# A four-layer graph network on one core: casting DMAs for the adjacency, eleven-block groups in the first layer, and paired row maxima in the second

## The chip, the core and the metric

The kernel runs on one core of one Trainium2 chip. The metric is device time in microseconds (us) of one execution; lower is better. TensorE is called PE below, VectorE DVE, ScalarE ACT, GpSimd POOL, and SyncE SP. SP issues nearly all DMAs of the kernel before.

## The reference, cut to what matters

The input is x (2708 x 256) and a 0/1 adjacency matrix adj (2708 x 2708, diagonal 1). Each of four layers computes `h = relu(layernorm(x))` and adds the result of a graph layer to x.

```
# layer 0: attention with 4 heads of 64 columns
ht = (h @ Wm) per head; el = ht.al; er = ht.ar
scores = leaky_relu(el[i] + er[j], 0.2), -inf where adj[i, j] == 0
x += softmax(scores) @ ht
# layer 1: two GRU cells and 3 attention heads; D = diag(adj), A = adj without its diagonal
edge_output = gru(A @ h, h)
hW = h @ W[k]; e = leaky_relu((A @ hW) . a)           # one score per node
support = mean over k of (softmax_j(e[j] where A[i, j] > 0) * A) @ hW
x += D * edge_output + D * gru(support, h)
# layer 2
x += concat(h, adj @ h / (deg + 1)) @ W2.T
# layer 3: its weights are not zero only where adj < 1 is not 0; for this input a flag skips it
```

## The kernel before, in words

Nodes are padded to 2816 = 22 tiles (`NT`) of 128. AT holds adj transposed in fp8, for all 22 source tiles j; most other buffers lie in one `arena` that the stages use in turn.

**Start.** DVE, ACT and PE normalise x and form ht and the two scores. SP loads adjT in 32-bit chunks into four staging buffers (`STG`), and POOL casts them into AT (L690 for the first six target blocks, L714 for the rest). Between the first casts POOL also splits six weight pieces into fp16 halves (L673 to L675). Then a chain over the 22 tiles forms MOV, the moving operand of layer 0: POOL L704 and DVE L1161 make the products, ACT L856 and DVE L1167 split them in two fp16 parts.

**Layer 0.** leaky_relu has two pieces, so exp of a score is a product of a row factor and a column factor, with different factors on either side of the threshold el + er > 0. A unit is (group g of target blocks, head h): `GA` has groups of 6, 8 and 8 blocks, thus 12 units. For each unit and each source tile j a threshold tile is made (0 or 1 in fp8 over the group's columns) by ACT as a steep sigmoid (L866), or for `j % 7 == 3` by DVE (L1183). DVE ands it with the AT words (`positive_mask`, L1215) and xors for the complement (`other_mask`, L1221), 4 bytes per word, into a ring of `NMASK` = 12. PE multiplies each mask block with MOV (L1677, 65 columns, 4 matmuls per block and tile j) into one PSUM bank per block. The first four and last four tiles j of a unit are taken together (`rounds(4)`). At j = 8 of the next unit ACT scales each bank by the row factors into E (`evict`, L878, two instructions a block), and two masks later DVE adds, divides and adds to X (`head_out`, L1230 to L1236). DVE also widens AT from 1 to 1.875 (`widen`, L1242), and POOL clears AT's diagonal blocks (L720).

**Before layer 1.** After the last unit: head_out, the last 8 blocks' `norm_stats` and `norm_scales` (L1084 to L1106), then a chain per tile: ACT norm (L824), POOL fp16 part (L727), DVE rest (L1284), PE transposes (L1694). ACT may start block t >= 8 only when SP has saved block t - 8 to DRAM (L515, one of eight buffers).

**Layer 1, edge GRU.** For each tile t PE does the support A @ h (L1723), the three heads' products (L1735, L1737) and the gates (L1768, L1775). ACT and DVE split the products (`products_low`, L1358), which PE waits for before the next tile's products. DVE also takes row maxima, `row_max`, one per head, tile and half row (132 in all, L1373): SP loads 1408 columns of adj in 32 bits (L506, three buffers `AROW`), POOL clears the diagonal block (L748), and DVE multiplies with the scores in EB and takes the maximum. 44 maxima of head 0 are spread over tiles 0 to 12 and 29 of head 1 over tiles 14 to 21; the other 59 lie in the attention stage.

**Layer 1, attention.** Nine units (3 heads x 3 groups). ACT or DVE make exponents (L960, L1416) from the row maxima MB, DVE masks them (L1426), ACT turns them into powers (L969), PE multiplies (L1818, L1819). MB comes from DRAM (`m_rows`): PE turns the maxima, DVE copies them (L1386), SP saves them (L542) and loads them broadcast (L551). The last stages are the node GRU, layer 2's linear part, and the neighbours' sum (L1872).

SP's program is one order of loads and waits; a wait holds up all that SP issues behind it. [The functions that the change touches follow.]

Of the kernel before, what the change touches and what calls it, by code (L numbers as in the profile page):

```python
# [6 lines left out]
F32 = mybir.dt.float32  # L7
# [8 lines left out]
P = 128  # L16


def gnn_stack_kernel(nc, t_in, out):
# [14 lines left out]
    H1 = 3  # L34
# [6 lines left out]
    GA = [(0, 6), (6, 8), (14, 8)]  # L41
# [3 lines left out]
    EVICT_AT = 8  # L45
    NTHR = 6
    NORM0_SPLIT = 4
    LOG2E = 1.0 / float(np.log(2.0))
# [5 lines left out]
    NORM1 = [(0, 14), (14, NT)]  # L54
# [8 lines left out]
    ROWS_SPLIT = 13  # L63
    ROWS_EDGE = 73
# [12 lines left out]
    with ExitStack() as ctx:  # L77
# [53 lines left out]
        THR = a0.take(NTHR, 1024, dt=FP8, size=1)  # L131
        mask_at = a0.at
        MASK = a0.take(NMASK, 2, 1024, dt=FP8, size=1)
        stg_at = a0.at
        STG = a0.take(4, 1024)
        stg_end = a0.at
        ELB = a0.take(2, 1024)
        e_at = a0.at
        E = a0.take(8, 2 * C0)
# [16 lines left out]
        RD = a0.take(8)  # L156
# [4 lines left out]
        assert a0s.at <= stg_at  # L161
        GWT = THR.rearrange("p a b -> p (a b)").bitcast(F32).rearrange("p (a b) -> p a b", b=D)
        htf_at = GA[0][1] * P
        HTF = AT[:, :, htf_at:htf_at + 4 * H0 * C0].bitcast(F32)
        THRi = THR.bitcast(mybir.dt.int32)
# [8 lines left out]
        EB = a1.take(N)  # L174
        AROW = a1.take(3, QUARTER)
        rows_end = a1.at
        NSH = a1.take(2, DC, 2, 2 * P, dt=F16, size=2)
        assert a1.at >= stg_at
        WIHS = a1.take(DC, 2, 3 * D, dt=F16, size=2)
        WHHS = a1.take(DC, 2, 3 * D, dt=F16, size=2)  # L180
        assert a1.at <= stg_end
# [4 lines left out]
        ah.at = late_at  # L186
        H32R = ah.take(8, D)
# [80 lines left out]
        M2 = sb("M2", [P, NT, 2, H1])  # L268
# [4 lines left out]
        KM = ln[:, 5, :]  # L273
# [4 lines left out]
        MN_D = nc.dram_tensor("m_rows", [H1, NT, P], F32, kind="Internal").ap()  # L278
        HT_D = nc.dram_tensor("h_turned", [P, NT, 4 * P], F16, kind="Internal").ap()
# [11 lines left out]
        banks_before = []  # L291
        cnt = 0
        for g, h in units0:
            banks_before.append(cnt)
            cnt += GA[g][1]
        banks_before.append(cnt)
        stg_before = [16 * len(range(q, len(chunk0), 4)) for q in range(4)]

        def threshold_on_act(n, j):

            if n == 0:
                return True
            return j % 7 != 3

        act_thr, dve_thr = [0], [0]
        for n in range(len(units0)):
            for j in range(NT):
                on_act = threshold_on_act(n, j)
                act_thr.append(act_thr[-1] + on_act)
                dve_thr.append(dve_thr[-1] + (not on_act))  # L310
# [37 lines left out]
        casts_at = {}  # L348
        n = NT
        for u, count in enumerate((6, 6, 5, 5, 6, 6, 5, 5)):  # L350
            for i in range(count):
                casts_at[(u, 1 + 4 * i if i < 2 else 10 + 3 * (i - 2))] = n
                n += 1
        assert n == len(chunk0)

# [4 lines left out]

        def rows_before(t):

            if t <= ROWS_SPLIT:
                return -(-2 * NT * t // ROWS_SPLIT)
            if t >= NT:
                return ROWS_EDGE
            return 2 * NT + max(0, -(-(ROWS_EDGE - 2 * NT) * (t - ROWS_SPLIT - 1) // (NT - ROWS_SPLIT - 1)))

        row_at = {2 * i: ROWS_EDGE + i for i in range(2 * NT * H1 - ROWS_EDGE)}
# [4 lines left out]
        def row_of(L):  # L374

            h, i = divmod(L, 2 * NT)
            return h, i // 2, i % 2
# [11 lines left out]
        first_count = [[0], [0], [0]]  # L389
        for m in range(3 * 3 * NT):  # L390
            for e in range(3):
                first_count[e].append(first_count[e][-1] + (first_of(m) == e))
        first_sem = ["y_act", "y_dve", "y_pool"]
# [20 lines left out]
        def _(sp):  # L414
# [4 lines left out]
            def load_chunk(n):  # L419
                g, j = chunk0[n]  # L420
                b0, nb = GA[g]
                if 4 <= n < NT + 4:
                    sp.wait_ge(sem("stg_cast"), n - 3)
                if n >= NT + 4:
                    sp.wait_ge(sem("stg_used"), n - 3 - NT)
                sp.dma_start(STG[:, n % 4, 0:nb * P], adjT[j, :, b0 * P:(b0 + nb) * P]
                             ).then_inc(sem(f"stg{n % 4}"), 16)

            def load_el(n):
                g, h = units0[n]  # L430
                b0, nb = GA[g]
                if n >= 2:
                    sp.wait_ge(sem("t_act"), act_thr[(n - 1) * NT])
                    if dve_thr[(n - 1) * NT] > 0:
                        sp.wait_ge(sem("t_dve"), dve_thr[(n - 1) * NT])
                sp.dma_start(ELB[:, n % 2, 0:nb * P].rearrange("p (k q) -> p k q", q=P),
                             EL_D[b0:b0 + nb, h, :].partition_broadcast(P)).then_inc(sem(f"elb{n % 2}"), 16)
# [17 lines left out]
            for n in range(4):  # L455
                load_chunk(n)
# [6 lines left out]
            for n in range(4, NT):  # L463
                load_chunk(n)
                i, odd = divmod(n - 5, 2)
                if odd == 1 and 0 <= i < len(pieces):
                    sp.wait_ge(sem("ws"), i + 1)
# [1543 lines left out]
```

## Time and profile before

| | |
|---|---|
| median of 3 runs | 1348.96 us (1347.34 to 1359.39) |
| the profiled execution's own time | 1352.68 us |
| its span, first to last instruction | 1350.9 us |
| PE, DVE, ACT, POOL busy | 1147.0, 975.3, 808.1, 322.4 us |
| mean granted clock of TensorE | 0.934 |

The profile is of one execution. Its own time is 1.8 us longer than its span and 3.7 us above the median. In it x = 0 is the first instruction; the stages follow each other at about 0 to 98 (start), 98 to 389 (layer 0), 389 to 450 (norm and scores of layer 1), 450 to 709 (edge GRU), 709 to 1068 (attention), 1068 to 1250 (node GRU) and 1250 to 1351 us (neighbours' sum).

### The profile page before, as it was taken

Reading aid. Unit: us, or ns where it says so; the run is one execution under the profiler, and the core shown is the slowest. Engines: PE = TensorE matmul, PEld = TensorE weight load, DVE = VectorE, ACT = ScalarE, POOL = GpSimd, SP = SyncE. Lnnn points to the kernel's source line nnn. Section 1 sums busy time; section 2 is a strip of 40 time slices with the busy share of each in tenths; the row PEclk is TensorE's granted clock in tenths of the full one; section 3 lists DMA queues with packets and bytes.
Section 4 is the critical chain, followed back from the end, with each engine's and each line's share of the span. In section 5 each row is a group of like instructions: output and inputs, shape, how many; then the busy total and the mean of one; then the engine's idle time right before and its main releaser. Section 6 shows DMA issues by size and latency. Waiting matters only on the chain.

```text
span 1350.9 us, 35958 instructions
## 1 busy us (share of the span) xinstructions
PE 1147.0 (85%) x15055; PEld 940.4 (70%) x15055; DVE 975.3 (72%) x2219; ACT 808.1 (60%) x1232; POOL 322.4 (24%) x383
## 2 busy tenths in 40 slices
PE   4518888999867999899966999999899997778997
PEld 3418888999757767666635888887788663445886
DVE  6599897899983577776786999897996365553541
ACT  3468889999753223223325999997989465653000
POOL 4862313133032032333231121111211042220000
PEclk9759999999975999999987999999899998899999
DMA  9734535111016577777779778776762010020532
GB/s 315 244 137 122 179 126 191 36 35 66 4 57 230 160 237 240 240 252 253 266 265 347 221 272 325 240 249 222 255 222 112 1 32 17 16 94 1 174 127 85
DMA packets 89465, 225.10 MB, mean 167 GB/s; under 512 B 7521, under 2 KB 52689, under 8 KB 89041
## 3 DMA queue, kind: packets, MB, share of 16 engines
q1 hardware_dynamic: 88113, 222.21, 48.8%
q8 instruction: 120, 1.97, 0.6%
q10 hardware_dynamic: 1184, 0.53, 0.1%
q14 instruction: 48, 0.39, 0.1%
HBM read 202.98 MB, written 19.73 MB: 165 GB/s over the span
## 4 chain that ended last, share of the span: by engine, by line
PE 38%; DVE 23%; DMA 17%; ACT 8%; issue 7%; POOL 5%; SPq 2%; DVEq 0%; ACTq 0%; POOLq 0%
DMA arena<-in_adj 14%; PE PS L1872 8%; PE PS L1818 7%; PE PS L1819 7%; PE PS L1677 6%; DVE scratch L1373 5%; DVE arena L1215 4%; PE PS L1768 3%; DVE arena L1221 3%; ACT arena L866 2%; PE PS L1859 2%; DVE arena L1161 2%; PE PS L1775 1%; ACT arena L878 1%; POOL arena L748 1%
## 5 line engine op out<-in xcount | busy, mean ns | idle before, releaser
L1818 PE MATMUL PS<-arena 128*128 128x257 f16 x1452 | 331.5, 276 | 21.4 <-ACT arena L969 14.7
L1819 PE MATMUL PS<-arena 128*128 128x257 f16 x1452 | 331.3, 277 | 0.0
L1677 PE MATMUL PS<-arena 128*128 128x65 f16 x7744 | 259.4, 195 | 75.8 <-DVE arena L1221 61.0
L1677 PEld LDWEIGHTS PS<-arena 128*128 128x128 fp8e4 x7744 | 255.3, 99 | 79.9 <-issue 58.0
L1373 DVE CUSTOM_DVE_ANT_0 scratch<-arena 128x1408 bf16<-128x1408 f32 x132 | 216.0, 1636 | 76.7 <-DMA arena<-in_adj 39.8
L866 ACT ACTIVATE arena<-arena 128x1024 fp8e4<-128x1024 f32 (+1 forms) x231 | 227.9, 1085 | 23.0 <-DVE arena L1215 22.5
L969 ACT ACTIVATE arena<-arena 128x896 int16<-128x896 uint8 (+1 forms) x198 | 187.6, 973 | 31.6 <-DVE arena L1426 22.3
L1818 PEld LDWEIGHTS PS<-arena 128*128 128x128 bf16 x1452 | 144.3, 99 | 47.4 <-ACT arena L969 13.6
L1819 PEld LDWEIGHTS PS<-arena 128*128 128x128 bf16 x1452 | 141.5, 97 | 23.0
L960 ACT ACTIVATE arena<-arena,E1B 128x896 uint8<-128x896 f32 (+1 forms) x131 | 139.3, 1064 | 12.7 <-DMA arena<-m_rows 12.7
L1215 DVE TENSOR_TENSOR arena<-arena,AT 128x256 int32<-128x256 int32 (+1 forms) x264 | 114.7, 434 | 26.2 <-ACT arena L866 26.1
L948 ACT ACTIVATE arena<-arena 128x256 f32<-128x256 f32 x44 | 18.3, 417 | 179.6 <-DVE arena L1397 179.6
L1768 PE MATMUL PS<-arena 128*128 128x512 f16 x528 | 122.9, 383 | 0.3 <-ACT PS L932 0.3
L1221 DVE TENSOR_TENSOR arena<-arena,AT 128x256 int32<-128x256 int32 (+1 forms) x264 | 116.3, 441 | 0.0
L748 POOL TENSOR_TENSOR arena<-arena,NOTI 128x128 f32<-128x128 f32 x66 | 47.3, 716 | 275.6 <-DMA arena<-in_adj 275.6
L1723 PE MATMUL PS<-AT,arena 128*128 128x256 fp8e4 x968 | 111.8, 276 | 0.0
L1872 PE MATMUL PS<-arena,AT 128*128 128x256 f16 x968 | 106.2, 273 | 0.8 <-DVE X L1523 0.8
L1723 PEld LDWEIGHTS PS<-AT,arena 128*128 128x128 f16 x968 | 95.6, 99 | 12.2
L1872 PEld LDWEIGHTS PS<-arena,AT 128*128 128x128 fp8e4 x968 | 94.6, 98 | 12.5 <-DVE X L1523 1.1
L733 POOL TENSOR_TENSOR arena<-arena 128x256 f32<-128x256 f32 x44 | 33.5, 761 | 258.1 <-ACT arena L948 258.1
L1768 PEld LDWEIGHTS PS<-arena 128*128 128x128 f16 x528 | 52.0, 99 | 57.3 <-issue 3.6
L1426 DVE TENSOR_TENSOR arena<-arena,AT 128x224 int32<-128x224 int32 (+1 forms) x198 | 82.3, 441 | 11.3 <-ACT arena L960 11.3
(187 smaller groups left out, 1537.8 us busy)
## 6 DMA issues: line engine op xcount, KB each, us to landing
arena<-in_adj SPq DMA_DIRECT2D x176, 704.0 KB, 5.4
arena<-in_adjT SPq DMA_DIRECT2D x44, 512.0 KB, 7.5
hw_saved<-arena SPq DMA_DIRECT2D x22, 387.0 KB, 7.2
arena<-in_adjT SPq DMA_DIRECT2D x22, 384.0 KB, 5.4
arena<-hw_saved SPq DMA_DIRECT2D x9, 774.0 KB, 7.9
arena<-h_saved SPq DMA_DIRECT2D x44, 128.0 KB, 2.1
arena<-e_rows SPq DMA_DIRECT2D x3, 1408.0 KB, 7.2
arena<-el_rows SPq DMA_DIRECT2D x8, 512.0 KB, 5.5
```

What stands on the lines that cost most here:

```text
L866: act.activation(THR[:, m % NTHR, 0:nb * P], ELB[:, n % 2, 0:nb * P], ACT.Sigmoid, bias=ERB[:, j, h:h + 1], scale=SHARP, saturate=False).t ...
L960: act.activation(Y[:, m % NRING, 0:nb * P], MB[n % 2][:, 0:nb * P], ACT.Relu, bias=E1B[:, j * H1 + h:j * H1 + h + 1], saturate=False).then ...
L969: act.activation(PWb[:, m % NRING, 0:nb * P], Y[:, m % NRING, 0:nb * P], ACT.Copy, scale=256.0).then_inc(sem("p_ready"), 1)
L1215: dve.tensor_tensor(mask_words(m, 0), THRi[:, m % NTHR, 0:GA[g][1] * P // 4], adj_words(m), ALU.bitwise_and).then_inc(sem("m_plus"), 1)
L1221: dve.tensor_tensor(mask_words(m, 1), mask_words(m, 0), adj_words(m), ALU.bitwise_xor).then_inc(sem("masks_built"), 1)
L1373: dve.tensor_tensor_reduce(junk, AROW[:, L % 3, :], eb[:, c * QUARTER:(c + 1) * QUARTER], 1.0, 0.0, ALU.mult, ALU.max, M2[:, t, c, h:h + 1 ...
L1677: ins = pe.matmul(PS[:, k, q * C0:(q + 1) * C0], MASK[:, (m + j) % NMASK, q, k * P:(k + 1) * P], MOV[:, j, 2 * h + q, a, :], start=(j == 0 ...
L1723: ins = pe.matmul(PS[:, c, 0:D], HHL[:, j, a, c * P:(c + 1) * P], AT[:, j, i0 * P:i1 * P], start=(j == 0 and a == 0), stop=(j == NT - 1 an ...
L1768: ins = pe.matmul(PS[:, bank, :], half(c, a), w[:, c, b, 0:2 * D], start=False, stop=(w is wih and c == DC - 1 and a == 1), skip_group_che ...
L1818: pe.matmul(PS[:, k, 0:D + 1], weights, w[:, 0:D + 1], start=(j == 0), stop=False)
L1819: ins = pe.matmul(PS[:, k, 0:D + 1], weights, w[:, D + 2:2 * D + 3], start=False, stop=(j == NT - 1))
L1872: ins = pe.matmul(o, AT[:, j, t * P:(t + 1) * P], YHL[:, j, a, :], start=(j == 0 and a == 0), stop=(j == NT - 1 and a == 1))
```

## The change

- **Loads.** Staging and POOL's casts go. POOL issues DMAs that cast while they move: 22 of adjT's first 11 blocks per tile (32 bits to fp8) at the start, 22 of the other 11 blocks, each after every third mask (masks 1 to 64), and then 22 DRAM-to-DRAM copies of adj's rows into a bf16 array `AH_D`, one every fourth mask from mask 68 to 152. POOL's six weight splits come after the first 22 issues. SP waits for the 22 copies, then writes zeros on the diagonal of AH_D with one DMA of 127 x 22 elements of 2 bytes, and waits for that too. Behind these waits on SP's queue are the loads of the GRU weights, the biases and the saves of h (L515).
- **Layer 0.** Two groups of 11 blocks, 8 units. A unit uses one of two sets of four PSUM banks, three blocks to a bank. ACT takes all 176 thresholds of 1408 columns and no evictions. DVE takes the masks of 352 words and, at j = 13, four evictions (three blocks each, one multiplication by a broadcast factor) and head_out for 11 blocks. The diagonal is cleared by two DVE ands at the end. After the last unit eviction, head_out and norm_stats go bank by bank; 11 blocks' norm_stats stand there instead of 8.
- **Row maxima.** One bf16 half row (352 KB, two buffers) serves heads 0 and 1: 44 loads for 88 maxima, spread over tiles 0 to 19 of the edge GRU; the maxima of both are turned and saved together. Head 2's 44 maxima and loads lie in the attention stage, at every 2.25th mask, and are turned at unit 5, j = 0 instead of j = 13. POOL's clearing of rows goes. The 26 checks in the attention stage have own buffers.

```diff
-    GA = [(0, 6), (6, 8), (14, 8)]
+    GA = [(0, 11), (11, 11)]
...
-    EVICT_AT = 8
+    EVICT_AT = 13
+    PER_BANK = 3
+    L0_BANKS = 4
...
-    NORM1 = [(0, 14), (14, NT)]
+    NORM1 = [(0, 11), (11, NT)]
...
-    ROWS_SPLIT = 13
-    ROWS_EDGE = 73
+    ROWS_LAST = 20
...
+        EB = a1.take(2, N)
+        AROW = a1.take(2, QUARTER, dt=BF16, size=2)
...
         def rows_before(t):
+            return min(PAIRED, -(-PAIRED * t // ROWS_LAST))
...
+        row_at = {8 + 9 * i // 4: 2 * NT + i for i in range(2 * NT)}
...                                                       SP
-            sp.wait_ge(sem("stg_used"), len(chunk0) - NT)
+            sp.wait_ge(sem("rows_h"), 16 * NT)
+            sp.dma_start(AH_D.rearrange("t p n -> (t p n)")[0:(P - 1) * NT * (N + 1)]
+                         .rearrange("(a b c) -> a b c", b=NT, c=N + 1)[:, :, 0:1],
+                         ZB[0:P - 1, :].unsqueeze(2), allow_slow_non_contiguous=True).then_inc(sem("rows_z"), 16)
+            sp.wait_ge(sem("rows_z"), 16)
             for i in range(4):
                 sp.wait_ge(sem(f"ws_out{i}"), 16 * len(range(i, len(pieces), 4)))
-            load_halves(WIHS, 1, "we")
-            load_halves(WHHS, 2, "we")
...
-            sp.wait_ge(sem("x_l0"), len(units0))
+            sp.wait_ge(sem("x_l0"), FULL0)
+            load_halves(WIHS, 1, "we")
+            load_halves(WHHS, 2, "we")
             load_bias(BIAS, BRB, "edge_bih", "edge_bhh", "be")
...
-                if L >= 3:
-                    sp.wait_ge(sem("rmax"), L - 2)
-                sp.dma_start(AROW[:, L % 3, :], t_in["adj"][t * P:(t + 1) * P, c * QUARTER:(c + 1) * QUARTER]
+                if L >= 2:
+                    sp.wait_ge(sem("rmax"), maxima_after(L - 2))
+                sp.dma_start(AROW[:, L % 2, :], AH_D[t, :, c * QUARTER:(c + 1) * QUARTER]
...
-                if n == 5 and j == 15:
-                    save_maxima(2)
+                if n == 5 and j == 2:
+                    save_maxima(2, 1)
...                                                       POOL
             for t in range(NT):
-                pool.wait_ge(sem(f"stg{t % 4}"), 16 * (t // 4 + 1))
-                pool.tensor_copy(AT[:, t, 0:GA[0][1] * P], STG[:, t % 4, 0:GA[0][1] * P], saturate=False
-                                 ).then_inc(sem("stg_cast"), 1)
...
+                pool.dma_start(AT[:, t, 0:GA[0][1] * P], adjT[t, :, 0:GA[0][1] * P]).then_inc(sem("adj_a"), 16)
+            for i in range(len(pieces)):
+                pool.wait_ge(sem(f"raw{i % 4}"), 16 * (i // 4 + 1))
+                if i >= 4:
+                    pool.wait_ge(sem(f"ws_out{i % 4}"), 16 * (i // 4))
+                split(RAW[:, i % 4, :], HALF[:, i % 4, :, :], pieces[i][3], 3 * D)
...
+            for t in range(NT):
+                pool.wait_ge(sem("masks_built"), 3 * t + 1)
+                pool.dma_start(AT[:, t, GA[0][1] * P:NT * P], adjT[t, :, GA[0][1] * P:NT * P]).then_inc(sem("adj_b"), 16)
+            for t in range(NT):
+                pool.wait_ge(sem("masks_built"), 68 + 4 * t)
+                pool.dma_start(AH_D[t], t_in["adj"][t * P:(t + 1) * P, :]).then_inc(sem("rows_h"), 16)
...                                                       DVE
+                dve.wait_ge(sem("t_act"), m + 1)
+                if h == 0 and j == 0:
+                    dve.wait_ge(sem(["adj_a", "adj_b"][g]), 16 * NT)
...
+            def evict(n, i):
...
+                dve.tensor_tensor(E[:, k0:k1, :].rearrange("p k (q c) -> p k q c", c=C0),
+                                  PS[:, first_bank(n) + i, 0:nb * 2 * C0].rearrange("p (k q c) -> p k q c", q=2, c=C0),
+                                  coef.to_broadcast([P, nb, 2, C0]), ALU.mult).then_inc(sem("bank_free"), 1)
...
+                if n >= 1 and j == EVICT_AT:
+                    for i in range(L0_BANKS):
+                        evict(n - 1, i)
+                    head_out(n - 1, 0, 11, L0_BANKS)
...
+            dve.tensor_tensor(blocks, blocks, not_diagonal.unsqueeze(1).to_broadcast([P, NT - 1, P // 4]), ALU.bitwise_and
+                              ).then_inc(sem("diag0"), 1)
...
+            for i in range(L0_BANKS):
+                k0, k1 = bank_blocks(i)
+                evict(len(units0) - 1, i)
+                head_out(len(units0) - 1, k0, k1, i + 1)
+                dve.wait_ge(sem("x_l0"), len(units0) + i)
+                for k in range(k0, k1):
+                    norm_stats(1, GA[1][0] + k)
...
+            def row_max(i):
+                if i < PAIRED:
+                    L, h = divmod(i, 2)
+                    eb = EB[:, h, :]
+                else:
+                    L, h = i - 2 * NT, 2
+                    eb = EB2
...                                                       PE
+                    for k in range(11):
+                        i, r = divmod(k, PER_BANK)
+                        if js[0] == 0 and n >= 2 and r == 0:
+                            pe.wait_ge(sem("bank_free"), L0_BANKS * (n - 2) + i + 1)
...
-                    if (n, js[-1]) in ((1, 12), (5, 9)):
+                    if (n, js[-1]) == (4, 19):
```

## Rows read from the trace of the kernel before

**Rows 1.** Busy time by stage: us, each engine's busy (count), PEclk, DMA share, GB/s

```profile
194.00:389.00 195.00, 177.48 (x5312) 175.40 (x5309) 176.38 (x465) 173.30 (x265) 50.38 (x35) 0.96 0.18 60
450.00:709.00 259.00, 233.14 (x1680) 164.71 (x1677) 186.11 (x339) 75.14 (x170) 72.60 (x95) 0.97 0.75 249
709.00:738.00 29.00, 17.53 (x108) 13.17 (x109) 16.19 (x29) 15.30 (x17) 4.88 (x8) 0.71 1.02 358
936.00:958.00 22.00, 14.98 (x110) 11.51 (x108) 16.40 (x35) 15.20 (x16) 3.34 (x3) 0.84 0.80 297
958.00:980.00 22.00, 22.00 (x200) 19.20 (x198) 22.00 (x35) 21.30 (x23) 5.12 (x3) 1.00 0.76 250
```

**Rows 2.** The same view for L1677 alone (PE, PEld), two 4 us windows of layer 0

```profile
234.00:238.00 4.00, 4.00 (x86) 4.00 (x83) 0.57 0.51 151
242.00:246.00 4.00, 4.00 (x132) 4.00 (x129) 1.00 0.01 4
```

**Rows 3.** ACT's timeline: start, us, what, forms, count [idle before]

```profile
91.28 13.41 ACT L866 ACTIVATE arena<-arena 128x768 fp8e4<-128x768 f32 x16
262.43 13.62 ACT L866 ACTIVATE arena<-arena 128x1024 fp8e4<-128x1024 f32 x13
205.60 3.35 ACT L878 ACTIVATE arena<-PS,arena 128x65 f32<-128x65 f32 x16
```

**Rows 4.** DVE's timeline: two masks back to back, and the last mask of layer 0

```profile
203.07 0.42 DVE L1215 TENSOR_TENSOR arena<-arena,AT 128x256 int32<-128x256 int32 x1
203.41 0.43 DVE L1221 TENSOR_TENSOR arena<-arena,AT 128x256 int32<-128x256 int32 x1
382.85 0.42 DVE L1221 TENSOR_TENSOR arena<-arena,AT 128x256 int32<-128x256 int32 x1
```

**Rows 5.** DVE's timeline: first of head_out, first norm_stats, variance, first of the chain

```profile
389.62 0.70 DVE L1230 TENSOR_TENSOR arena<-arena 128x520 f32<-128x520 f32 x1 [3.46 <-ACT arena L878]
392.25 0.43 DVE L1084 BATCH_NORM_STATS2 scratch<-X 128x6 f32<-128x256 f32 x1
396.62 0.17 DVE L1091 TENSOR_SCALAR ln<-mv 128x8 f32<-128x8 f32 x1
398.34 0.42 DVE L1284 TENSOR_TENSOR arena<-arena 128x256 f16<-128x256 f32 x1
```

**Rows 6.** POOL's timeline: last constant, one weight split, first product of the MOV chain

```profile
16.35 0.29 POOL L687 CAST identh<-ident 128x128 f16<-128x128 f32 x1
20.24 0.84 POOL L673 TENSOR_SCALAR arena<-arena 128x768 f32<-128x768 f32 x1 [2.06 <-DMA arena<-in_gatW]
23.63 0.82 POOL L690 CAST AT<-arena 128x768 fp8e4<-128x768 f32 x1
60.52 1.77 POOL L704 TENSOR_TENSOR arena<-AT,arena 128x260 f32<-128x260 f32 x3
```

**Rows 7.** SP's timeline, a load's issue; DMA view, 8 to 10 us, ACT's queue

```profile
0.73 0.45 SPq L416 DMA_DIRECT2D X<-in_x  x1
...
q10 hardware_dynamic: 181, 0.00, 4.9%
```

**Rows 8.** Who waited for whom in the edge GRU: us, times, longest

```profile
PE PS L1735 <- DVE arena L1358: 25.6, 12, 4.5
DVE scratch L1373 <- DMA arena<-in_adj: 38.5, 13, 4.7
```

**Rows 9.** Timeline of the edge GRU: PE's products of two tiles, a second maximum

```profile
560.17 0.39 PE L1735 MATMUL PS<-arena 128*128 128x512 f16 x1 [1.94 <-DVE arena L1358]
570.85 0.39 PE L1735 MATMUL PS<-arena 128*128 128x512 f16 x1
579.97 1.62 DVE L1373 CUSTOM_DVE_ANT_0 scratch<-arena 128x1408 bf16<-128x1408 f32 x1 [0.17 <-DVE M L1373]
```

**Rows 10.** Attention: PE's first matmul (timeline), a save of maxima (chain of waits)

```profile
716.65 0.38 PE L1818 MATMUL PS<-arena 128*128 128x257 f16 x1 [7.94 <-ACT arena L969]
...
929.15 3.84 DMA m_rows<-ET
```

More of the change, by code:

```diff
@@ L155, in gnn_stack_kernel @@
         ELT = a0.take(P)
-        RD = a0.take(8)
+        RD = a0.take(11)
+        ZB = a0.take(NT, dt=BF16, size=2)
+        NOTB = a0.take(P, dt=FP8, size=1)
         a0s = Arena()
@@ L290, in gnn_stack_kernel, with bank_blocks, first_bank @@
         chunk3 = [(g, j) for g in range(len(G0)) for j in range(NT)]
[L291 to L310, printed above, removed]
+        FULL0 = len(units0) + L0_BANKS - 1
+        def bank_blocks(i):
+            return PER_BANK * i, min(PER_BANK * (i + 1), 11)
+        def first_bank(n):
+            return L0_BANKS * ((n + 1) % 2)
+        stg_before = [0] * 4
         norm_parts = {0: NORM0, 1: NORM1, 2: NORM2, 3: [(0, NT)]}
@@ L1257, in _ @@
                     widen(j - 2, 1)
[L1258 to L1259 removed]
                 if m >= 1:
                     other_mask(m - 1)
[L1262 to L1263 removed]
+                if n >= 1 and j == EVICT_AT:
+                    for i in range(L0_BANKS):
+                        evict(n - 1, i)
+                    head_out(n - 1, 0, 11, L0_BANKS)
                 if n == len(units0) - 2 and 3 <= j < 3 + NORM1[0][1]:
                     if j == 3:
[L1266 removed]
+                        dve.wait_ge(sem("x_l0"), H0)
                     norm_stats(1, j - 3)
@@ L1270, in _ @@
             other_mask(last)
+            norm_scales(1, 0)
             dve.wait_ge(sem("masks_built"), last + 1)
@@ L1273, in _ @@
                 widen(t, 1)
-            norm_scales(1, 0)
-            head_out(len(units0) - 1)
-            dve.wait_ge(sem("x_l0"), len(units0))
-            for t in range(*NORM1[1]):
-                norm_stats(1, t)
+            dve.wait_ge(sem("widened"), 2 * NT)
+            not_diagonal = NOTB.bitcast(mybir.dt.int32)
+            flat = AT[:].rearrange("p t n -> p (t n)").bitcast(mybir.dt.int32)
+            blocks = flat[:, 0:(NT - 1) * (N + P) // 4].rearrange("p (t c) -> p t c", t=NT - 1)[:, :, 0:P // 4]
+            dve.tensor_tensor(blocks, blocks, not_diagonal.unsqueeze(1).to_broadcast([P, NT - 1, P // 4]), ALU.bitwise_and
+                              ).then_inc(sem("diag0"), 1)
+            block = flat[:, (NT - 1) * (N + P) // 4:NT * N // 4]
+            dve.tensor_tensor(block, block, not_diagonal, ALU.bitwise_and).then_inc(sem("diag0"), 1)
+            for i in range(L0_BANKS):
+                k0, k1 = bank_blocks(i)
+                evict(len(units0) - 1, i)
[3 more added lines that the diff above has]
+                    norm_stats(1, GA[1][0] + k)
             norm_var(1, 1)
@@ L1388, in gru_new, with maxima_turned @@
+            def maxima_turned(h, heads, bank):
+                dve.wait_ge(sem("eT_mm"), 2 if h < 2 else 3)
+                dve.wait_ge(sem("ep") if h == 0 else sem("mn"), 16)
+                dve.tensor_copy(ET[0:heads * NT, :], PS[0:heads * NT, bank, 0:P]).then_inc(sem("mt"), 1)
             def gru_new(t, base, trz, gt):
```

333 lines of the change are left out of this document (113 added, 220 removed).

## The prediction

> **What bounds the kernel now.** I read the stages first (busy time by stage), then the timelines of the engines in each. In layer 0 no engine is idle for long: in 194 to 389 us, eight units of 8 blocks, PE is busy 177, DVE 176 and ACT 173 of 195 us, 24.4 us a unit [rows 1]. Undisturbed, PE does 132 matmuls in 4 us, 30.3 ns each; in the window after a gap the granted clock is 0.57, near the lower level of 1.2 GHz, and it does 86, 46.5 ns each [rows 2]. A unit of 8 blocks needs 704 matmuls, 21.3 us at full clock. ACT needs 19 thresholds at 13.62/13 = 1.05 us and 16 evictions in 3.35 us, 23.3 us [rows 3]. So ACT sets the pace, and the stage runs 24.4/23.3 = 1.045 times slower than ACT's work.
>
> In the edge GRU PE is busy 233 of 259 us, and 25.6 us of its waits are for DVE's split of the products (L1358), which is late because DVE stood at row maxima whose row was not there [rows 1, 8]. In the attention PE is nearly full, except in two places: 709 to 738 us, with DMA at 1.02 and 358 GB/s, and 936 to 958 us, where it waits for the maxima of head 2 [rows 1, 10].
>
> **Layer 0, the thresholds.** From 768 to 1024 columns a threshold goes from 13.41/16 = 0.84 to 1.05 us; 384 columns more make 1.363. 22 are 30.0 us a unit [rows 3]. ACT loses all evictions. **PE:** 968 matmuls a unit, the total stays 7744, 29.3 us [rows 2]. It no longer waits for evictions, having a second set of banks. **DVE:** masks of 256 words follow each other by 0.34 us; 352 words make at most 0.46 (in proportion), I take 0.44. 44 are 19.4. Four evictions of at most 390 columns: a 520-column add takes 0.70, so about 0.5 each, 2.0. head_out took 392.25 - 389.62 = 2.63 us for 8 blocks, 3.5 for 11 [rows 4, 5]. Together 24.9 us. Widening adds 7 x 0.45 = 3.1 in units 4 to 6. Unit 6 also has 11 norm_stats at (396.62 - 392.25)/8 = 0.55, thus 34.0; unit 7 has 22 widenings, 34.8 [rows 5]. So ACT leads in units 0 to 5, DVE in 6 and 7: 6 x 30.0 + 68.8 = 249 us, times 1.045 = 260. Before, from the first threshold at 91.28 to the last mask at 383.3, it was 292.0 [rows 3, 4]. With 1.4 for the first threshold: **31 us gained**; 42 if the factor is 1. A window at the low clock costs PE 46 matmuls, 1.4 us; two in each unit make 22 us, of which PE's lead of 0.7 us a unit covers 6, and the gain is 15 [rows 2].
>
> **After layer 0.** Before, the first step of the tile chain (L1284) came 15.1 us after the last mask [rows 4, 5]. Now DVE has norm_scales, two widenings and the two ands (about 4 us), then per bank an eviction (0.5), head_out of three blocks (five short operations, 1.6) and three norm_stats (1.65), 3.75 x 3 + 2.8, then variance and scales, 398.34 - 396.62 = 1.7. Sum 20: **5 us lost**. PE's last round (176 matmuls, 8.2 us at 46.5 ns) lies beside it. POOL's clearing of AT was off this path, so its end gives nothing.
>
> **The start.** POOL comes to the MOV chain at 60.5 us now; its inputs would allow about 55. It will issue 22 casting loads from 16.6 us on, then six splits of 3.4 us (20 us) [rows 6]. The trace has no DMA issued by POOL. An issue on SP takes 0.45 us [rows 7]; as low bound 16.6 + 10 + 20 = 47, 5 us gained; a split is three POOL instructions, 1.1 us each, and the high bound is twice that: 16.6 + 48 + 20 = 85, 24 lost. I take the 1.1 us of the same engine: 61 us, plus waits for pieces: **3 lost**. The 22 loads read 15.9 MB. At the 358 GB/s of the saturated stage [rows 1] they take 44 us and end near 61 to 75 beside the other loads; they delay the first mask only under about 215 GB/s. The second 22 have 88 masks (some 125 us), and are hidden. On POOL's queue nothing is behind them but the row copies.
>
> **Row copies and diagonal.** 31.7 MB are read and 15.9 written between masks 68 and 152, about 195 to 322 us, 250 GB/s of reads; the last lands near 328. Then come 2794 elements of 2 bytes. ACT's small loads (4 bytes) held the engines 4.9% of 16 x 2 us for 181 packets, 8.7 ns each [rows 7]: 2 us over 16 engines, 24 us on one. The saves of h wait behind on SP, and ACT's ninth block needs the first at about 374 us. So 46 us, 16.5 ns a packet, are free: **0**, low bound 0. A 2-byte write to DRAM is not in the trace; at five times the read price on one engine it takes 122 us, 76 lost. I stay with the packets' own row. The Trainium skill (DMA: Bandwidth & Descriptors, "Why a DMA increments its semaphore by 16 and not by 1") says that the number of engines is the largest up to 16 that divides the slowest dimension, and 127 partitions go to one. By that rule the zeros take the 24 us rather than 2; no row here shows it. "Specifications" there adds that transfers under 512 bytes are read-modify-write; no row prices that either.
>
> **Edge GRU.** A tile that did not wait took PE 570.85 - 560.17 = 10.7 us; 22 are 235 against 259 [rows 1, 9]. Loads fall from 73 of 704 KB to 44 of 352, so rows will be there. But DVE's maxima rise from 73 to 88, 4.4 a tile at 1.62 to 1.79 us [rows 9], 7.3 us; bf16 input alone I count at nothing, since the scores stay 32 bits. DVE's other work was 186.1 - 73 x 1.7 = 62, 2.8 a tile [rows 1, 9], and I allow 0.9 for waits within DVE's chains: 11.0 in tiles 0 to 19. So 20 x 11.1 + 2 x 10.7 = 243, plus 4 for the start: **12 gained**; 20 if DVE hides wholly, 0 if every 5-maxima tile (12 us) delays PE.
>
> **Attention.** A full stretch gives 22/200 = 0.11 us a matmul. Of 709 to 738, 29 us, PE needed 108 x 0.11 = 12: 17 lost [rows 1]. Its 7.94 us wait at 716.65 ended a chain of save, load and exponents that began when DVE copied the turned maxima in tile 20, late by its waits for head 1's rows. Tiles 20 and 21 now have no maxima, and 2.1 MB of rows loaded beside the chain become 0.7. I take 13 of the 17. 936 to 958 did 110 instead of 200: 10 lost, since the save began at 929 [rows 1, 10]. It moves 13 tiles ahead, some 20 us: 9 back. **22 gained**, 10 to 27.
>
> **Sum.** 31 - 5 - 3 + 0 + 12 + 22 = 57, from 1352.7 to 1295.7 for this execution; the runs' median is 3.7 lower. I say **1295**, 54 off the median, a little short of the sum since waits between full engines show only when reached.
>
> **Rivals.** (a) **The cover is thinner:** layer 0 gives 15, the edge GRU 0 to 5 and the start costs 10, with the rest as above: 1352.7 - (15 - 5 - 10 + 3 + 22) = 1328. For: PE and ACT are within 3% of each other, and DVE passes PE in the edge GRU. Against: ACT has no wait for PE left. (b) **Slower: the casts and the zeros hold SP.** Casting DMAs were never in the trace. At 150 GB/s the first mask comes at 17 + 106 = 123, 31 late; the row copies take 211 us from 226 on, to 437; with 24 us of zeros SP is free at 461, where ACT wants it at 374 + 31 = 405: 56 more. 57 - 31 + 3 - 56 = -27, 1380 us. At 165 GB/s gain and loss cancel. Fast casts with zeros at over 37 ns a packet (2794 x 37 = 103 us, 57 past the free 46) do the same. Against: plain loads reach 358. (c) **POOL pays for its issues:** 2.2 us each, 24 lost at the start instead of 3: 1295.7 + 21 = 1317. (d) **Two row buffers instead of three:** each of 44 loads comes 0.4 us late, 17 us, edge GRU -5 instead of 12: 1313.
>
> **How the numbers follow.** Forecast (1270 to 1312): 0.55. (a) 0.12, (b) and its slow zeros 0.15, (c) and (d) 0.12, all else 0.06. 1275 is the sum with the clean layer 0 and edge GRU (11 + 8 more); 1350 takes in (a), (c), (d) and the mild part of (b). Within 1% (13.5 us, about what runs tell apart) is 1335.5 to 1362.5: the mild part of (b) and the worst of (a), 0.08. Slower 0.13, faster 0.79.
>
> **What would show it.** Thresholds 1.36 us apart; DVE masks under 0.46 us; PE's L1677 from about 100 to 363 us; L1284 first at about 369; SP's L515 right behind head_out, with the zeros' DMA ended before. Wrong, if POOL's first L704 is past 70, adjT lands past 90, or ACT waits for saves. In the edge GRU PE's waits for L1358 should fall under 12 us. In the attention no wait over 3 us for m_rows.

## The result, and the profile after

The changed kernel takes **1335.5 us** (median; 1332.7 to 1336.1) against 1350.5 for the kernel before on the same chip: ratio 0.987, 95% interval 0.982 to 0.992. So 15 us are gained where 54 were forecast. The profiled execution has a span of 1332.9 us against 1350.9. Marks that both traces have, the first or last start of a PE line, split these 18.0 us (e_mm are the 484 matmuls that give the node scores of layer 1; the mark is the first of them):

| stretch | before, us | after, us | gained | forecast |
|---|---|---|---|---|
| start, to layer 0's first matmul | 97.9 | 93.2 | 4.7 | -3 |
| layer 0, first to last matmul | 290.9 | 300.1 | **-9.2** | **31** |
| from there to e_mm (L1712, now L1654) | 30.9 | 35.8 | -4.9 | -5 |
| e_mm to the edge GRU's last gates | 287.5 | 280.4 | 7.1 | 12 |
| from there to the last attention matmul | 356.3 | 336.5 | 19.8 | 22 |
| the rest | 287.4 | 286.9 | 0.5 | 0 |

Only layer 0 is far off, by 40 us, and the wrong way. The stages of the kernel after answer to [rows 1]:

```profile
93.00:394.00 301.00, 259.06 (x7744) 256.43 (x7744) 219.70 (x495) 237.55 (x176) 23.42 (x44) 0.97 0.53 83
394.00:429.00 35.00, 16.29 (x220) 13.28 (x220) 24.92 (x80) 17.03 (x32) 10.86 (x23) 0.54 0.61 203
465.00:711.00 246.00, 224.18 (x1614) 157.63 (x1612) 219.80 (x372) 73.43 (x167) 60.54 (x61) 0.98 0.41 116
711.00:730.00 19.00, 14.52 (x113) 11.40 (x113) 8.41 (x18) 15.73 (x18) 4.41 (x5) 0.91 0.89 301
730.00:1047.00 317.00, 313.61 (x2798) 270.05 (x2795) 259.37 (x531) 287.61 (x314) 24.83 (x18) 1.00 0.48 157
```

In layer 0 no engine is full: PE idles 42 of 301 us, ACT 63, DVE 81. The three views of waits (PE, DVE, ACT; 95 to 392 us) say who holds whom:

```profile
PE PS L1619 <- issue: 41.3, 23, 3.6
```

```profile
DVE arena L1130 <- PE PS L1619: 63.3, 31, 6.4
DVE arena L1130 <- ACT arena L811: 15.5, 26, 4.4
```

```profile
ACT arena L811 <- DVE arena L1130: 51.1, 21, 5.4
```

ACT waits for DVE to free a threshold, DVE for PE to free a mask, and PE for nothing that the profile shows ("issue"), 23 times. PE's timeline in one such stretch, with the count of matmuls:

```profile
224.90 4.26 PE L1619 MATMUL PS<-arena 128*128 128x65 f16 x128 [3.21 <-issue]
232.75 5.70 PE L1619 MATMUL PS<-arena 128*128 128x65 f16 x128 [3.58 <-issue]
238.95 0.23 PE L1619 MATMUL PS<-arena 128*128 128x65 f16 x2 [0.51 <-issue]
```

Between two such waits lie 128 matmuls or a multiple, to within one. PE does 128 in 4.26 us at a granted clock of 1.00 (224.90 to 229.16 us), and in 5.70 us at 0.70, a mean over both levels, right behind the wait of 3.58 us. The profile's list of queues (packets, MB, share of 16 engines) says what comes in such portions:

```profile
q1 hardware_dynamic: 74993, 127.05, 30.8%
q0 software_dynamic: 7392, 23.79, 12.9%
q8 instruction: 120, 1.97, 0.6%
```

1.97 MB in 120 packets is 16 KB each. PE's 15054 matmuls and as many weight loads, 30108 instructions, over 120 packets are 251 each, so I take a packet of q8 as a block of 256 instructions, 128 matmuls with their weights. In layer 0 alone (DMA view, 93.2 to 393.3 us) the 7744 matmuls go with 61 packets, 127 each:

```profile
q8 instruction: 61, 1.00, 1.3%
```

PE uses up a block every 4 us there. The DMA view of the same 15 us (224 to 239) shows what else the DMA engines had to do:

```profile
q0 software_dynamic: 144, 2.16, 68.5%
q1 hardware_dynamic: 686, 0.34, 15.1%
q8 instruction: 2, 0.03, 0.7%
```

q0 holds the row copies, q1 an el_rows broadcast. This gives the theory **F (fetch)**: PE waits for its own instructions, which come late while the DMA engines work on the row copies, the casts of adjT and the broadcasts.

The trace also has the start and duration of each packet. PE ran dry at 221.69 and at 229.17 us; the next q8 packets started only at 222.46 and 230.39 us, and PE went on at 224.90 and 232.75. The DMA views of 222.4 to 222.5 and 230.3 to 230.5 us show them, 0.96 and 0.89 us of one engine:

```profile
q8 instruction: 1, 0.02, 60.1%
q8 instruction: 1, 0.02, 27.9%
```

All 23 waits end 2.2 to 2.5 us after a q8 packet has started. Where PE does not wait, in e1 and e10 below, the packet mostly starts 3.1 to 3.9 us ahead of its matmuls. No q8 packet in layer 0 takes over 1.6 us. So a block is late because its packet starts late, not because it moves slowly.

The kernel before had such waits too, ten with 12.4 us in all from 98 to 389 us; two of them in PE's timeline:

```profile
119.30 4.25 PE L1677 MATMUL PS<-arena 128*128 128x65 f16 x128 [2.61 <-issue]
...
208.92 22.00 PE L1677 MATMUL PS<-arena 128*128 128x65 f16 x640 [1.78 <-issue]
```

Rivals of F: **B**, the new order of banks and groups makes the waits; **E**, the el_rows broadcasts alone (packets of 512 bytes) make them.

### The profile page after: what moved, and what is told of

The parts are those of the page before. It is cut to its first block, busy times and chain, and to the rows that moved or that the text cites. A ratio compares the mean times of both kernels' runs of the same rounds, so it can differ in the third digit from the quotient of the medians.

```text
span 1332.9 us, 35106 instructions
## 1 busy us (share of the span) xinstructions
PE 1140.3 (86%) x15054; PEld 938.5 (70%) x15054; DVE 937.4 (70%) x2037; ACT 785.0 (59%) x1001; POOL 216.7 (16%) x296
## 3 DMA queue, kind: packets, MB, share of 16 engines
q8 instruction: 120, 1.97, 0.6%
## 4 chain that ended last, share of the span: by engine, by line
PE 56%; DVE 23%; issue 8%; ACT 6%; DMA 3%; POOL 3%; ACTq 0%; SPq 0%; DVEq 0%; POOLq 0%
PE PS L1619 18%; PE PS L1760 10%; PE PS L1761 10%; DVE scratch L1316 9%; PE PS L1814 8%; PE PS L1710 3%; POOL arena L703 2%; PE PS L1801 2%; DVE arena L1298 2%; DVE arena L1090 2%; PE PS L1717 1%; PE PS L1587 1%; DMA arena<-e_rows 1%; DVE arena L1342 1%; PE PS L1654 1%
## 5 line engine op out<-in xcount | busy, mean ns | idle before, releaser
L1760 PE MATMUL PS<-arena 128*128 128x257 f16 x1452 | 325.5, 272 | 7.6 <-ACT arena L897 4.4
L1619 PE MATMUL PS<-arena 128*128 128x65 f16 x7744 | 259.1, 196 | 80.8 <-issue 41.3
L1761 PE MATMUL PS<-arena 128*128 128x257 f16 x1452 | 325.5, 274 | 0.0
L811 ACT ACTIVATE arena<-arena 128x1408 fp8e4<-128x1408 f32 x176 | 242.5, 1456 | 51.4 <-DVE arena L1130 51.1
L1316 DVE CUSTOM_DVE_ANT_0 scratch<-arena 128x1408 bf16<-128x1408 bf16 x132 | 223.2, 1691 | 23.7 <-DMA arena<-e_rows 11.1
L1760 PEld LDWEIGHTS PS<-arena 128*128 128x128 bf16 x1452 | 142.7, 98 | 32.6 <-issue 8.6
L1761 PEld LDWEIGHTS PS<-arena 128*128 128x128 bf16 x1452 | 139.9, 96 | 21.5
L1130 DVE TENSOR_TENSOR arena<-arena,AT 128x352 int32<-128x352 int32 x176 | 91.3, 519 | 83.4 <-PE PS L1619 63.3
L1710 PE MATMUL PS<-arena 128*128 128x512 f16 x528 | 122.3, 382 | 0.4 <-ACT PS L860 0.4
L703 POOL TENSOR_TENSOR arena<-arena 128x256 f32<-128x256 f32 x44 | 47.4, 1076 | 377.8 <-ACT arena L876 377.8
L1814 PEld LDWEIGHTS PS<-arena,AT 128*128 128x128 fp8e4 x968 | 94.6, 98 | 12.5 <-DVE X L1466 1.1
L1710 PEld LDWEIGHTS PS<-arena 128*128 128x128 f16 x528 | 51.8, 98 | 56.8 <-issue 2.7
L1136 DVE TENSOR_TENSOR arena<-arena,AT 128x352 int32<-128x352 int32 x176 | 90.8, 516 | 0.0
L1423 DVE SCALAR_TENSOR_TENSOR scratch<-arena 128x1408 fp8e4<-128x1408 f32 x44 | 73.2, 1664 | 0.8 <-DMA arena<-in_adj 0.8
## 6 DMA issues: line engine op xcount, KB each, us to landing
arena<-el_rows SPq DMA_DIRECT2D x8, 704.0 KB, 11.5
```

The lines of the kernel that those rows point to most:

```text
L811: act.activation(THR[:, m % NTHR, :], ELB[:, n % 2, :], ACT.Sigmoid, bias=ERB[:, j, h:h + 1], scale=SHARP, saturate=False).then_inc(sem("t ...
L1130: dve.tensor_tensor(mask_words(m, 0), THRi[:, m % NTHR, :], adj_words(m), ALU.bitwise_and).then_inc(sem("m_plus"), 1)
L1136: dve.tensor_tensor(mask_words(m, 1), mask_words(m, 0), adj_words(m), ALU.bitwise_xor).then_inc(sem("masks_built"), 1)
L1316: dve.tensor_tensor_reduce(junk, AROW[:, L % 2, :], eb[:, c * QUARTER:(c + 1) * QUARTER], 1.0, 0.0, ALU.mult, ALU.max, M2[:, c, h * NT + t ...
L1619: ins = pe.matmul(PS[:, first_bank(n) + i, (2 * r + q) * C0:(2 * r + q + 1) * C0], MASK[:, (m + j) % NMASK, q, k * P:(k + 1) * P], MOV[:, ...
L1710: ins = pe.matmul(PS[:, bank, :], half(c, a), w[:, c, b, 0:2 * D], start=False, stop=(w is wih and c == DC - 1 and a == 1), skip_group_che ...
```

## The experiments

The runs come from several chips. On the chip of e1 to e4 the kernel before took 1348.9 us, of e5 to e8 1351.3, of e9 and e10 1353.1, of e11 1352.3; the kernel after ran where it took 1350.5. Medians of different groups compare only to within these few us. Times of a stage are from one profiled execution each.

**e1, all casts ahead of layer 0.**

```
-                pool.wait_ge(sem("masks_built"), 3 * t + 1)      # before each cast of adjT's second columns
...
-                pool.wait_ge(sem("masks_built"), 68 + 4 * t)     # before each row copy
...                                                       DVE
                 if m == 0:
+                    dve.wait_ge(sem("adj_b"), 16 * NT)
+                    dve.wait_ge(sem("rows_h"), 16 * NT)
```

> Both sets of 22 casting DMAs (second columns of adjT, row copies) are issued before layer 0, and DVE's first mask waits for all of them; nothing is left out. Theory F (fetch): PE's 23 waits in layer 0 that nothing in the profile releases (41.3 us), each after a multiple of 128 matmuls, are waits for its own instruction blocks (queue q8, 16 KB each), which come late while the DMA engines work on casting packets. Then nearly all of these waits go, and first threshold to last mask falls from 301 us to 255 to 265 (ACT's 8 x 30 plus the widening units). The start grows by about 145 us (44 casts at 3.3 us of all engines), so the run is 1335 + 145 - 40 = 1440. Rival B (banks and grouping): the waits belong to the new order of matmuls and banks; the stage stays at 301 and the run is 1480. Rival E (broadcasts): the el_rows loads of 1408 packets of 512 B cause them; then waits stay around the six loads inside the stage, about 285 us.

Measured: 1402.1 us. PE's line in layer 0 (duration ns min/median/max, first and last start), its waits in 204 to 455 us, and the stage:

```profile
L1619 PE MATMUL PS<-arena x7744: 191/193/247, 203.1 to 456.2; 128*128 128x65 f16 x199
```

```profile
PE PS L1619 <- issue: 4.0, 4, 2.4
```

```profile
203.00:457.00 254.00, 249.02 (x7744) 248.31 (x7744) 216.04 (x492) 231.60 (x173) 0.00 (x0) 0.99 0.10 21
```

The matmuls take 253.1 us instead of 300.1, with the same banks, groups and broadcasts: B falls, and so does E: the broadcasts alone leave 4.0 us of waits. Of the 47 us, 37 are waits that are gone, and 10 are PE's busy time, 259.1 to 249.0 for the same 7744 matmuls: after waits the granted clock was lower (0.97 as a mean, now 0.99). The run is 38 us under the expected 1440. The casts end sooner (the delay to the first matmul is 110 us, not 145), and the stage gains 7 more than the 40 written down.

**e2, only the row copies ahead of layer 0.** The same wait, for `rows_h` alone; the casts of adjT stay paced.

> Only the 22 row copies are moved ahead of layer 0 (DVE's first mask waits for them); the casting loads of adjT stay paced by masks. Theory F: the 17 unreleased waits of PE after 189 us (32 us, at the time of the row copies) go, those before (6, 9 us, at the time of the adjT casts) stay: the stage falls from 301 to about 268, the run is 1335 + 73 - 33 = 1375. Rival B: stage 301, run 1408. Rival E: waits stay near the el_rows loads, stage 285 to 295.

Measured: 1376.0 us.

```profile
L1619 PE MATMUL PS<-arena x7744: 190/193/247, 167.3 to 433.2; 128*128 128x65 f16 x199
```

Layer 0 is 265.9 us. The unreleased waits are 8.0 us (7) up to 263 us, beside the casts of adjT, and 3.8 (3) after it; in the kernel after they were 7.7 (5) up to 189 us and 32.2 (17) from there to 355. So the copies cost 34 us, and the casts of adjT with what is left about 13 (265.9 against e1's 253.1).

**e3, short packets.**

```
-                pool.dma_start(AH_D[t], t_in["adj"][t * P:(t + 1) * P, :]).then_inc(sem("rows_h"), 16)
+                for c in range(2):
+                    pool.dma_start(AH_D[t, :, c * QUARTER:(c + 1) * QUARTER], ...same columns of adj...)
```

> Each row copy is issued as two halves of the columns, so its packets (on average 14 KB written, 1.1 us each, as DRAM to DRAM rows are contiguous) can be at most 2.8 KB written; bytes and pace stay. If an instruction block waits behind the packet that an engine is working on (theory F in its form 'length of packet'), the row copies' 32 us of waits shrink to a third or less: run 1335 - 20 = 1315. If it waits for its share of busy engines whatever the packet (F, 'share'), or by B or E, nothing changes: 1335.

Measured: 1328.1 us, layer 0 292.8 us. The packets of q0 are now 0.23 us long on average (6489 in 58.7% of 16 engines, 190 to 350 us), a fifth of what they were, 1.11 us (1203 in 52.4%). The waits beside the copies are as many (17) but 26.5 us instead of 32.2; the longest is 3.6 us in both. The run as a whole does not show the gain: its ratio to the kernel before is 0.986 (0.983 to 0.990), that of the kernel after 0.987 (0.982 to 0.992). So the first form of F, 20 us by the length of a packet, falls, and the 7 us of layer 0, from one trace each, are a hint only.

**e4, a flat el_rows.** el_rows holds the row scores in DRAM; each broadcast load of it now reads one row of 5632 bytes instead of eleven pieces of 512, and it is written by 22 small DMAs instead of one. (The later waits on the semaphore were left as they were here; from the last attention matmul to the end is 286 us, in the kernel after 287.)

```
-        EL_D = nc.dram_tensor("el_rows", [NT, H0, P], F32, ...)
+        EL_D = nc.dram_tensor("el_rows", [H0, NT, P], F32, ...)
-                sp.dma_start(ELB[...].rearrange("p (k q) -> p k q", q=P), EL_D[b0:b0 + nb, h, :].partition_broadcast(P))
+                sp.dma_start(ELB[...], EL_D.rearrange("h t q -> h (t q)")[h, b0 * P:(b0 + nb) * P].partition_broadcast(P))
```

> el_rows is laid out head by head, so each broadcast load reads one contiguous row of 5632 bytes for each partition instead of eleven of 512. Theory F: 704 KB in 128 long packets hold the engines for about 2 us instead of 4.3; of the 41 us of waits up to 8 go: run 1328 to 1335. Rival E: most of the waits go, since the eleven-piece loads cause them: 1300. Rival B: 1335.

Measured: 1320.9 us, below my range of 1328 to 1335. The loads land in 6.7 us instead of 11.5, layer 0 takes 286.3 us, and the waits fall from 41.3 to 28.2 us. E is right in part: beside the other transfers the broadcasts in pieces are worth 14 us, two fifths of what the copies cost. The three amounts, 34, 13 and 14, add to more than the 47 of e1, which kept the broadcasts in pieces: part of each is due to their meeting, and they are not to be summed.

**e5, the row copies after layer 0.** Six follow mask 172, the others come one after another in the edge GRU's tiles, and the diagonal is cleared copy by copy.

```
+            pool.wait_ge(sem("masks_built"), 172)
+            send_rows(6)
             for t in range(NT + 1):
                 if t < NT:
                     delta(t, 0, HR, GT)
+                    send_rows(6 + 5 * (t + 1) // 4)
```

> The row copies leave layer 0: six are issued by POOL after mask 172, the others one after another in the tiles of the edge GRU, always some tiles ahead of their loads, and the diagonal is cleared copy by copy (128 elements each). Theory F (fetch): layer 0 runs as it did with the copies moved ahead, PE's 300 us become about 267, and the edge GRU, which needs only some 13 instruction blocks in 240 us, hides the copies: run 1335 - 30 = 1305. If the copies cost the edge GRU as much as they cost layer 0 (rows late, POOL held up at its issues), the run stays at 1335. Rival B (banks and grouping): layer 0 stays at 300, the run at 1335 or above.

Measured: 1312.4 us; layer 0 from 92.2 to 362.1, 269.9 us. The gain of layer 0 came as expected (30 us), and the run is 7 above the expected 1305: in the trace the stretch from e_mm to the edge GRU's last gates is 12.5 us longer than in the kernel after (292.8 against 280.3 to the last start of the gates' first line, L1710), and DVE now waits 14.9 us for rows.

**e6, plain copies at the old places.** The casting copies ahead, and at masks 68 to 152 the same rows once more in float32, DRAM to DRAM, into a tensor that nothing reads.

> As e2_rows_first (row copies ahead of layer 0), but at the masks where the row copies stood, the same rows are copied once more, plainly: float32 from DRAM to DRAM without a cast, by the same queue, into a tensor that nothing reads. Same reads, twice the bytes written. If casting is what delays the instruction blocks, PE's matmuls of layer 0 take 266 us as in e2 and the run is 1376. If any bulk transfer that fills the engines does it (theory F in its form 'share'), the unreleased waits after the 68th mask return: stage 290 to 305, run 1400 to 1415.

Measured: 1417.4 us.

```profile
L1624 PE MATMUL PS<-arena x7744: 190/194/247, 164.9 to 471.7; 128*128 128x65 f16 x199
```

```profile
PE PS L1624 <- issue: 42.8, 20, 6.3
```

306.8 us against e2's 265.9, just above the range that F gave. A cast is not needed for the waits: a plain bulk transfer at these places brings them back. It is not the same load, since it writes twice the bytes. The longest wait is 6.3 us instead of 3.6; a packet of q0 took 1.34 us on average (874 in 52.4% of 16 engines over 290 to 430 us) against 1.11 in the kernel after.

**e7, e5 with the flat el_rows.**

> e5_rows_late with the flat el_rows of e4_el_flat (the wait of layer 2 for its weights on the same semaphore raised by the added increments). Theory F: the two gains add as far as the waits differ: 33 from the copies and 3 to 6 of the waits that are left: PE's layer 0 260 to 263 us, run 1298 to 1302. If el's gain in e4 came only from its meeting the row copies, nothing is added: 1305.

Measured: 1308.0 us (1301.0 to 1312.3, six runs), above the expected 1298 to 1302. Layer 0 from 92.1 to 348.1, 256.0 us, is under the 260 to 263 expected. In the profiled executions 12.6 of these 14 us reach the end (span 1299.0 against 1311.6), but this one is the fastest of the six; the medians show 4, and the runs spread by 11 us.

**e8, e_rows flat as well**, saved by three DMAs `EP_D[h] <- ET[h:NT * H1:H1, :]`.

> e7_rows_late_el with e_rows laid out head by head too, so the two score loads ahead of the edge GRU read rows of 11 KB in place of 22 pieces of 512 bytes for each partition; it is saved by three DMAs instead of one. The profile after shows 13.0 us between the save and the first row maximum for two such loads, 7.0 before for one. By the edge GRU's own step (two loads of packets of 512 B are what delays its first maximum) 4 to 6 us go: 1293 to 1297. If the maxima have slack in the first tiles, nothing: 1300.

Measured: 1301.4 us, where I expected 1293 to 1297, and the trace does not bear out my reason: from e_mm to the first row maximum it is 38.3 us, against 35.8 in the kernel after, and DVE still waits 10.0 us for e_rows (11.1 in the kernel after). The span is e7's (1298.6 against 1299.0), and the 7 us between the medians lie within the spread of e7's runs. DVE's waits in the edge GRU (384 to 682 us) show what was given back since the copies moved there:

```profile
DVE scratch L1343 <- DMA arena<-adj_rows_half: 15.5, 5, 4.8
DVE arena L1376 <- POOL arena L729: 11.9, 17, 1.4
DVE scratch L1343 <- DMA arena<-e_rows: 10.0, 2, 8.3
```

The rows are late, and PE's waits for DVE's split are 29.6 us, against 21.2 in the kernel after.

**e9, copies further ahead:** `send_rows(13)` after POOL's halves of h, then `send_rows(14 + t)`.

> e8_all_flat with the row copies further ahead: seven more are issued once POOL has made the halves of h (about 394 us), the rest one for each tile, so 13 stand before the first tile instead of 6. In e8 DVE waited 15.5 us in the edge GRU for rows of adj_rows_half and PE 29.6 us for DVE's split of the products (21.2 in the kernel after). If these are late copies, PE's waits fall to 21 or less and the run from 1301 to 1292 to 1295. If the copies cost by sharing the DMA engines there, the run stays at 1300, and the e_mm matmuls (484, now 17 us) show new unreleased waits.

Measured: 1297.3 us, ratio 0.960 (0.957 to 0.963). DVE's wait for the rows falls to 4.9 us, PE's for the split to 23.6. I had expected 1292 to 1295 and at most 21 us of the latter. The other half of the expectation holds too: e_mm take 19.0 us from first to last instead of 16.8, with 5.8 us of unreleased waits (3.6 in e8). From its first matmul to the first gates it is 41.6 us instead of 36.0, and the tiles take 249.1 instead of 255.1, so in the traces the whole stretch gained nothing (290.8 against 291.1). The 4 us between the medians, from two chips, are not clear of noise: the ratios are 0.960 (0.957 to 0.963) and 0.964 (0.959 to 0.968).

**e10, the same in two halves.**

> e9_rows_lead with each copy issued as two halves of the columns. In layer 0 this took 7 us off, as PE's waits for instruction blocks grew shorter; after layer 0 PE needs few blocks, so by theory F nothing more is won: within 3 us of e9_rows_lead. POOL pays 0.5 us more at each copy, which lies beside its waits for ACT.

Measured: **1292.0 us**, ratio 0.957 (0.953 to 0.961), the fastest kernel here; the kernel after has 0.987. PE's line and waits in layer 0 (94 to 347 us):

```profile
L1650 PE MATMUL PS<-arena x7744: 191/193/247, 92.3 to 347.8; 128*128 128x65 f16 x199
```

```profile
PE PS L1650 <- issue: 4.1, 4, 1.8
```

It is 5 us better than e9, on the same chip, where I expected at most 3: from e_mm to the last gates it is 284.3 us instead of 290.8, and DVE waits 3.0 us for rows and PE 20.0 for the split. Layer 0 did not change (255.5 against 254.8), so this gain is not one of F's.

**e11, the kernel before with the flat el_rows.**

> The kernel before the change with el_rows laid out head by head (as e4_el_flat, the later waits on its semaphore raised). Its PE has 12.4 us of waits in layer 0 that nothing releases, while the plain loads of adjT and the el_rows broadcasts run. If the eleven- or eight-piece broadcasts delay instruction blocks there too, 3 to 6 us go from layer 0; but ACT, not PE, sets that kernel's pace there, so of the run at most these: 1345 to 1350. A gain of 10 or more, as in e4_el_flat, would say that the flat layout acts by something other than PE's blocks.

Measured: 1344.3 us, 8 below the kernel before and just under the expected 1345 to 1350, ratio 0.994 (0.992 to 0.997). Layer 0 is 283.9 us instead of 290.9, but the unreleased waits hardly fall (12.4 to 11.1 us from 98 or 100 us on). What the flat layout gives there is not PE's blocks alone, and this run does not say what it is; so for e4, too, F covers the 13 us of waits that went, and no more.

## Why the prediction was wrong

**Layer 0 is the step that failed:** "ACT leads in units 0 to 5, DVE in 6 and 7: 6 x 30.0 + 68.8 = 249 us, times 1.045 = 260". Its own prices were close. Six thresholds in the rows of the kernel after, 8.26 us, are 1.377 each (1.363 forecast), and masks follow each other at 0.44:

```profile
85.00 8.26 ACT L811 ACTIVATE arena<-arena 128x1408 fp8e4<-128x1408 f32 x6
```

```profile
383.34 0.52 DVE L1130 TENSOR_TENSOR arena<-arena,AT 128x352 int32<-128x352 int32 x1
383.77 0.52 DVE L1171 SCALAR_TENSOR_TENSOR AT<-AT 128x352 int32<-128x352 int32 x1
384.21 0.52 DVE L1136 TENSOR_TENSOR arena<-arena,AT 128x352 int32<-128x352 int32 x1
```

Undisturbed, the stage is near what the sum said, 249 or with the factor 260: 253 us of matmuls in e1, 256 in e7 and e10. What failed is a price of zero. I wrote of the second 22 casts that they "are hidden", and of the row copies, with the zeros behind them, "46 us ... are free: **0**": I looked for who waits for the data, the first mask and the saves of h, and not for who shares the DMA engines. PE's instructions do. The kernel before showed it: its ten unreleased waits, runs of 128 and 640 matmuls between them, and q8 in its list of queues; I took the factor 1.045 for all of it. Rival (a), "the cover is thinner", is nearest in time (1328) and had PE's low clock in it, but as a price of short gaps between full engines, at most 16 us. The measured loss is 40: 37 of waits (e1) and 10 of low clock, with the clean stage 7 better than my 260.

What the Trainium skill says bears on this ("DMA: Bandwidth & Descriptors", "Queues, rings and completion order"): each DMA engine serves its queues in turn and changes only between packets. e3 and e6 agree in direction only: with packets of 0.23 us instead of 1.11 the waits beside the copies are 26.5 us instead of 32.2, with packets of 1.34 us the longest is 6.3 instead of 3.6. But the block for 224.90 us started 4.5 us later than usual, by an estimate: 0.8 us after PE ran dry, where 3.7 us ahead is the median in e1 and e10. That is four packets of 1.1 us, so one packet of one other queue does not explain it, if the profile's packets are those that the rule means, which no view says.

**The start** was 7.7 us better than forecast: POOL issues its 22 casting loads in 12.00 us, 0.55 each. My low bound of 0.45 was nearly right and the 1.1 us that I took were twice too much; rival (c) fell with it.

```profile
15.99 12.00 POOL L666 DMA_DIRECT2D AT<-in_adjT  x22
```

**After layer 0** the sum of 20 us stands: DVE's last mask at 386.0 us, the tile chain's first L1224 at 405.6. The zeros, at price 0, were hidden indeed, and not by much:

```profile
353.41 0.81 SPq L466 DMA_DIRECT2D adj_rows_half<-arena  x1
...
402.70 0.82 SPq L463 DMA_DIRECT2D arena<-w_halves  x2
```

```profile
q1 hardware_dynamic: 2795, 0.01, 11.1%
```

2795 packets held 11.1% of the 16 engines from 353.5 to 387 us: 32 us in time where ACT's small loads gave 24 on one engine and 2 on sixteen [rows 7], and 16 us before SP has the next to do. The Trainium skill's rule quoted in the prediction ("DMA: Bandwidth & Descriptors", "Why a DMA increments its semaphore by 16 and not by 1") puts them on one engine. The trace is near what it gives: 32 us, a packet every 10 ns (median), and never more than two in progress at a time. The sum of their durations is 1.8 times the stretch, but that does not count engines, since durations overlap elsewhere too (the share of 16 engines was 1.02 in the 29 us at 709 [rows 1]). Rival (b) was never near. ACT waited for a save of h once, 1.95 us; 1.5 MB of GRU weights now load right ahead of the saves, and no run tests that as the cause.

**The edge GRU's** tiles took what I said: first to last gate 245.5 us, forecast 243. But the window I subtracted from, 259 us, began 7.3 us ahead of the first gates, for which I allowed 4, and PE's waits for the split fell to 21.2 us and not under 12. DVE is now nearly full (219.8 of 246 us), waits for POOL 14.3 us in all, and a row maximum takes it 1.73 us on average, where I had 7.3 us for 4.4 of them, 1.66 each; how much of PE's waits each makes was not tested. (The 11.0 us a tile of the prediction stand as 11.1 in its sum; with 11.0 it is 241 instead of 243.) Rival (d) did not show: DVE never waited for adj_rows_half.

**The attention** gave 19.8 of 22. Head 2's stall is gone (936 to 958 us: PE busy 21.7 of 22), and PE's first wait is 3.56 us instead of 7.94 [rows 10]. The load of m_rows ahead of it takes 4.62 us, of which ACT waits 2.04, so no wait for it is over 3, as I had said:

```profile
714.58 0.37 PE L1760 MATMUL PS<-arena 128*128 128x257 f16 x1 [3.56 <-ACT arena L897]
```

All terms but layer 0 add to 26 in the forecast and to 27 in the trace. That is in part luck: the start was 7.7 us better than forecast, the edge GRU 4.9 and the attention 2.2 worse.

**What stays open:** what holds a block's packet back until it starts. The trace shows its start and its end, not when it was asked for, and no run changed q8 itself. F is shown by taking each source away (e1, e2, e5) and putting one back (e6), by the 128, and by the q8 packet that starts 2.2 to 2.5 us ahead of the end of each wait. Open, too, are what the flat layout does in the kernel before (e11) and what the halves do in the edge GRU (e10).

## What to carry to other kernels

Before calling a transfer hidden, look at what else is fetched beside it: divide the matmuls by the packets of the instruction queue, and where an engine runs through a block in a few microseconds, do not price a bulk DMA beside it at nothing. The unreleased waits that the trace already has are a floor rather than a price: the kernel before had 12.4 us of them, the kernel after 7.7 up to 189 us, beside the casts, but 32.2 beside the row copies. Put background copies where few instructions run per microsecond: the same 22 copies cost 34 us in layer 0. In the edge GRU the stretch with them was 12.5 us longer than without when six stood ahead (e5), 10.5 with thirteen ahead (e9) and 4.0 with thirteen ahead in halves (e10).

## What was not expected of the hardware

- An instruction block (16 KB, by the counts above 256 instructions) that comes late stopped PE for up to 3.6 us in the kernel after and 6.3 in e6. After one such wait the matmuls ran at a granted clock of 0.70: 5.70 us for 128 instead of 4.26 at 1.00. Without the waits the same 7744 matmuls were busy 10 us less.
- The block's own packet takes 0.9 to 1.6 us in layer 0 of the kernel after; what comes late is its start. PE goes on 2.2 to 2.5 us after it.
- A broadcast load of 704 KB landed in 11.5 us in pieces of 512 bytes and in 6.7 us in rows of 5632 bytes, beside the same traffic.
- Copies from DRAM to DRAM have packets of 13 KB and 1.1 us if the rows are contiguous (1203 packets for 15.97 MB), and of 0.23 us in halves of the columns (e3).
